# Bidirectional selective scan with a routed FFN gate on one core: two more states scaled on ScalarE, two more products with C on GpSimd, and a new table of steps

## The reference

```
xn = layernorm(x)                                   # over channels
def scan(x, x_proj_w, dt_proj_w, dt_proj_b, A_log, Dp):
    A = -exp(A_log)                                 # 256 channels x 16 states
    delta, B, C = split(x @ x_proj_w.T)             # 32 + 16 + 16
    delta = softplus(delta @ dt_proj_w.T + dt_proj_b)
    h[t] = exp(delta[t]*A) * h[t-1] + delta[t]*B[t]*x[t]     # per channel and state
    return sum over states of h*C  + Dp*x
s = scan(xn, forward weights) + reverse(scan(reverse(xn), backward weights))
g = silu(xn + 0.3*(expert(xn) @ Wo + bo))           # one of 8 experts per batch: W2 @ gelu(W1 @ xn)
out = x + s*g
```

## Time and profile before

| | |
|---|---|
| profiled execution / its span | 3351.6 / 3349.7 us |
| TensorE busy | 2571.1 us, 77% |
| VectorE busy | 3109.2 us, 93% |
| ScalarE busy | 2909.8 us, 87% |
| GpSimd busy | 3010.5 us, 90% |
| DMA, share of 16 engines | 38.3% |
| mean granted clock of TensorE | 0.91 |

### The profile page before, as it was taken

One profiled execution on the slowest core, in us unless ns is written; L12 is line 12 of the kernel. 1 busy time (PEld: TensorE's weight loads), 2 busy tenths in 40 slices (PEclk: granted clock), 3 DMA queues, 4 the chain that ended last, 5 costly groups with the idle time before them and its releaser, 6 DMA issues. The chain is left out here.

```text
span 3349.7 us, 47861 instructions
## 1 busy us (share of the span) xinstructions
PE 2571.1 (77%) x15542; PEld 2055.5 (61%) x15542; DVE 3109.2 (93%) x2059; ACT 2909.8 (87%) x5370; POOL 3010.5 (90%) x1422
## 2 busy tenths in 40 slices
PE   7677777777778777777777787777787777778776
PEld 4566566666566666666665666665666666666665
DVE  2799999999999999999999999999999999999999
ACT  3898898988898898899888899988988988988885
POOL 0889999999999999999899999999999999999997
PEclk8898899889998988899898999889998988998898
DMA  5333434433434433434324444334344334344232
GB/s 171 112 110 94 131 121 129 127 106 96 139 121 128 125 99 105 136 120 128 114 87 131 126 132 125 107 98 131 121 128 125 105 99 138 121 129 125 95 104 70
DMA packets 273358, 394.09 MB, mean 118 GB/s; under 512 B 45003, under 2 KB 119508, under 8 KB 273108
## 3 DMA queue, kind: packets, MB, share of 16 engines
q1 hardware_dynamic: 273108, 391.03, 38.3%
HBM read 348.98 MB, written 25.18 MB: 112 GB/s over the span
## 5 line engine op out<-in xcount | busy, mean ns | idle before, releaser
L452 POOL TENSOR_TENSOR bx<-dx,b_sb 128x1024 f32<-128x1024 f32 x640 | 1514.5, 2386 | 75.9 <-DVE hs L798 75.3
L798 DVE TENSOR_TENSOR_SCAN hs<-decay,bx 128x1024 f32<-128x1024 f32 x640 | 1457.1, 2279 | 53.5 <-ACT decay L696 40.1
L1032 PE MATMUL y<-ident,hc 128*128 128x128 f32 x8192 | 1144.8, 291 | 29.1 <-DVE hc L776 29.0
L1032 PEld LDWEIGHTS y<-ident,hc 128*128 128x128 f32 x8192 | 1029.2, 152 | 144.6 <-DVE hc L776 85.7
L440 POOL TENSOR_TENSOR hc<-hs,c_sb 128x1024 f32<-128x1024 f32 x416 | 983.2, 2376 | 7.3 <-DVE hs L798 7.3
L798 DVE TENSOR_TENSOR_SCAN hs<-decay_sb,decay 128x1024 f32<-128x1024 f32 x384 | 864.8, 2273 | 76.9 <-issue 37.8
L699 ACT ACTIVATE decay<-delta,rate 128x512 f32<-128x512 f32 (+1 forms) x1280 | 827.2, 683 | 64.0 <-DVE hs L798 63.5
L776 DVE TENSOR_TENSOR hc<-hs,c 128x1024 f32<-128x1024 f32 x608 | 728.3, 1198 | 38.2 <-PE c L1015 32.4
L561 ACT ACTIVATE dxb<-dxT,btok 128x256 f32<-128x256 f32 x1536 | 651.1, 497 | 0.0
L1007 PE MATMUL decay<-ident,dxb 128*128 128x128 f32 x3072 | 443.7, 292 | 248.9 <-DVE hs L798 244.4
L1007 PEld LDWEIGHTS decay<-ident,dxb 128*128 128x128 f32 x3072 | 367.1, 149 | 363.7 <-issue 269.4
(11 more groups left out here) (127 smaller groups left out, 2287.7 us busy)
## 6 DMA issues: line engine op xcount, KB each, us to landing
b_sb<-b_scratch SPq DMA_DIRECT2D x640, 256.0 KB, 3.3
c_sb<-b_scratch SPq DMA_DIRECT2D x416, 256.0 KB, 3.5
xin<-in_L_attn_x_dram SPq DMA_DIRECT2D x32, 512.0 KB, 7.6
w_sb<-in_L_ffn_W_dram SPq DMA_DIRECT2D x32, 512.0 KB
w2o_sb<-w2o_scratch SPq DMA_DIRECT2D x32, 512.0 KB
xres<-in_L_attn_x_dram SPq DMA_DIRECT2D x32, 512.0 KB, 5.3
out_dram<-og SPq DMA_DIRECT2D x32, 512.0 KB, 4.3
dbc<-high SPq DMA_DIRECT2D x64, 128.0 KB, 5.4
```

The source lines that it names most:

```text
L452: nc.gpsimd.tensor_tensor(bx[:, i % RING, :, :], dx[:, g, :, :], b_sb[:, i % BRING, :].unsqueeze(1).broadcast_to([P, DT, T]), ALU.mult).th ...
L798: V.tensor_tensor_scan(hs[:, s % HSLOTS, :, :].rearrange("p k t -> p (k t)")[:, u], factor.rearrange("p k t -> p (k t)")[:, u], data.rearr ...
L1032: ins = M(yps[:, c, k * P:(k + 1) * P], hc[:, s % RING, k, c * P:(c + 1) * P], ident[:, :], start=False, stop=(s == ADDED[-1]), is_transpo ...
```

## The change

Only numbers of the table change. Two more states are `TURNED` (14 for 12: 20 and 26 come in; `POOL_B` falls from 20 to 18), and `POOL_C` grows from 13 to 15, other states than before among them; VectorE's products fall from 19 to 17 a row. `MEAN`, `SCALE`, `SHIFT` go from steps 0, 1, 4 to 1, 3, 5, the second `RATIO` from 30 to 35, the second `LOG1P` from 36 to 38, the first two `DX_COPY` from 30, 31 to 32, 33.

```diff
-    MEAN, SCALE, SHIFT, NORM = 0, 1, 4, 6
+    MEAN, SCALE, SHIFT, NORM = 1, 3, 5, 6
-    EXPAND, ABS = (14, 15, 24, 25), (16, 17, 26, 27)
-    EXP, LN, SQUARE, RATIO = (18, 27), (19, 28), (20, 29), (21, 30)
-    LOG1P, STEPSIZE, DX = (25, 36), (27, 39), (28, 43)
-    DX_TURN, DX_COPY = (28, 29, 44, 45), (30, 31, 46, 47)
-    FFN_IN, HIDDEN, GELU = (16, 16, 18, 18, 20, 20, 22, 22), (18, 20, 22, 24), 31
+    EXPAND, ABS = (14, 16, 26, 27), (17, 19, 29, 30)
+    EXP, LN, SQUARE, RATIO = (20, 30), (21, 31), (22, 34), (23, 35)
+    LOG1P, STEPSIZE, DX = (25, 38), (27, 40), (28, 43)
+    DX_TURN, DX_COPY = (28, 29, 44, 45), (32, 33, 46, 47)
+    FFN_IN, HIDDEN, GELU = (18, 18, 20, 20, 22, 22, 24, 24), (21, 23, 25, 27), 31
-    TURNED = (5, 6, 8, 9, 11, 13, 14, 15, 22, 24, 28, 30)
-    SCALED_AT = (0, 2, 3, 4, 5, 7, 9, 10, 17, 19, 23, 25)
+    TURNED = (5, 6, 8, 9, 11, 13, 14, 15, 20, 22, 24, 26, 28, 30)
+    SCALED_AT = (1, 2, 3, 4, 5, 7, 9, 10, 16, 17, 18, 20, 22, 24)
-    POOL_C = (2, 4, 5, 7, 9, 10, 11, 12, 16, 18, 20, 26, 27)
+    POOL_C = (1, 3, 5, 6, 9, 10, 11, 12, 14, 16, 18, 19, 20, 22, 26)
```

More of the change, by code:

```diff
@@ L47, in mamba_moe_block @@
     SKIP = {0: ((0, 0), (2, 0)), 1: ((0, 1), (1, 0), (1, 1), (2, 1)), 4: ((3, 0), (3, 1))}
-    TURNED, SCALED_AT, TURN_LEAD = (5, 6, 8, 9, 11, 13, 14, 15, 22, 24, 28, 30), (0, 2, 3, 4, 5, 7, 9, 10, 17, 19, 23, 25), 3
+    TURNED, SCALED_AT, TURN_LEAD = (5, 6, 8, 9, 11, 13, 14, 15, 20, 22, 24, 26, 28, 30), (1, 2, 3, 4, 5, 7, 9, 10, 16, 17, 18, 20, 22, 24), 3
     POOL_B = [s for s in range(STEPS) if s not in TURNED]
-    POOL_C, C_LAG, ADD_LAG = (2, 4, 5, 7, 9, 10, 11, 12, 16, 18, 20, 26, 27), 4, 2
+    POOL_C, C_LAG, ADD_LAG = (1, 3, 5, 6, 9, 10, 11, 12, 14, 16, 18, 19, 20, 22, 26), 4, 2
     ON_DVE = [s for s in range(STEPS) if s not in POOL_C]
```

## The result

The changed kernel takes 4025.74 us (median of four runs, 4022.52 to 4027.28), the kernel before 3361.25 us on the same chip (3357.11 to 3365.94): the ratio is 1.1966, 95% interval 1.1946 to 1.1987. The forecast was 3930 us with a range of 3710 to 4040. It is slower, by the loop that was forecast, and 96 us more than forecast. The profiled execution has a span of 4020.7 us.

What follows compares the result with a forecast made beforehand. VectorE was taken to bound the kernel, with 4.8 us idle a row. A row of 107.2 + 12.3 = 119.5 us, 18.5 over 101.0, gave +573 over 31 seams: 3925, plus 5.8, so 3930 us, range 3710 to 4040.

Steps and rivals of the forecast that it cites:

- the loop that was forecast: Late waits in series leading from one row to the next: a row of 119.5 us, 18.5 more than 101.0.
- T: The end of scan 0, from which the prediction counts its times; 1729.6 in the rows of before.
- seam: VectorE, end of scan 31 to end of the next row's scan 0: 12.3 us, where it was 6.35.
- step 2: GpSimd's small operations to the expansion of delta: transfers into dbc come later, expansion at T + 60.8 (58.7 to 64.9).
- the bound at the late end: The latest landing of a transfer into dbc in step 2, 8.5 us at most: 4058 us in all.
- Step 1: T to GpSimd's four small operations: rsq ready at T + 17.3, GpSimd waits 12.7 us, VectorE stalls 7 us.
- Step 3: Softplus of the first direction: RATIO ends at T + 84.3, GpSimd's LOG1P waits 5 us more.
- rival A: Faster: waits between engines give way, only VectorE's two products count; 98.7 us a row, 3286 us; chance 0.04.
- Rival B: Only the seam counts, GpSimd's list not late: +3.65 a row, 3470 us; chance 0.1, shared with one stall alone.
- C: Slower by GpSimd late from Step 1 and the seam, dbc and RATIO in time: 3770 us; chance 0.2.
- Rival D: TensorE becomes the bound, its clock falling in idle time: perhaps 2 to 3 us a row, 3990 to 4020; chance 0.1.
- The Trainium skill's drain behind a table load: About 1.38 us at each table load; by this rule seam 15.1, row 2.8 us longer; the forecast left it out.

Runs made afterwards that it cites:

- dbc_early: The changed kernel with SyncE's transfers into dbc issued ahead of the loads of C and of x: 3851.97 us.
- csd_log: copy_scale_dbc with the two LOG1P at 27 and 39 instead of 25 and 38 and the first STEPSIZE at 28: 3338.84 us, ratio 0.9921.
- copy_scale_dbc: The changed kernel with the first two dx copies at 31, 32, MEAN, SCALE, SHIFT at 0, 1, 4, and the edit of dbc_early: 3488.86 us.

## Why the prediction was right

**The mechanism** was right, and its places in time came out, up to the transfers into dbc and in the pieces behind them: T + 17.4 for the small operations (forecast 17.4), T + 27.8 for C product 3 (27.8), T + 53.4 for C product 12 (53.5), 22.8 us of softplus (22.7), a seam of 12.7 (12.3), and 23.1 us between the start of LOG1P at 1667.16 and the end of scan 31 (22.9). The experiments show the parts as causes and not only as rows: removed one by one and together they add.

**The size** was 96 us short, and the term that was mis-sized is in step 2: "a transfer lands 5.5 us after", of which I took 4.4 because there would be less traffic. That median is over all 128 transfers, but TensorE waits for the last of four, and in the row shown that took 7.2 us (1759.34 to 1766.56). The median of the fourth transfer alone, from issue to landing, is 6.9 us in the trace of the kernel before and 6.6 after, so the trace had it. The expansion came at T + 63.5 and not T + 60.8. ScalarE read the bank 1.2 us later and not 0.75, as TensorE's matmuls ran at a granted clock of 0.50 there (0.76 us for 0.48 at 1.00): it began at T + 64.7 in the row shown and not at T + 61.6. With 0.3 us more from LOG1P to the end of scan 31 and 0.4 at the seam, a steady row became 123.1 and not 119.5.

Two errors in the count of rows lie over this, of opposite sign. The first row also runs through the loop up to its own last operation, which came at 227.9 and not at 211.6: 16 us that "31 seams" left out. But the last of the 31 intervals, counted like the others, takes 97.0 us (92.0 before), since no front of a next row stands in it, and the one ahead of it 119.0: 23 us that the sum had too much. 29 x 3.6 - 23 + 16 = 97. That the last row hid 23 us of the miss is luck; the bound at the late end, 8.5 us for the transfer, held the rest.

**Step 1** had one thing hidden in it: undoing it alone gave 132 us and not 221, since the second RATIO, moved to 35, stands in the same step. The stall of 6.3 us at scan 7 had two causes, one behind the other. The prediction counted RATIO as a part of the delay of `rsq`, not as a wait of its own.

**Step 3** is borne out in kind. GpSimd's wait for RATIO was 7.4 us a row, (299.3 - 62.5)/32, where the prediction had 5.2 (T + 84.3 less T + 79.1). Of it 4.7 went with dbc_early: they were the late transfers. Only 2.7 are the two steps between RATIO and LOG1P by themselves. The 150 us of csd_log look like the forecast's 5.2 x 31 = 161, but csd_log moves both LOG1P, and the waits in copy_scale_dbc divide about evenly between the two. The second one is not in step 3; in the changed kernel it hides behind the wait for rsq.

**Busy time as the rival A read it** (98.7 us a row) didn't come in any kernel. The best, csd_log, has (3331.0 - 206.2)/31 = 100.8 us; of VectorE's 2.3 us fewer a small part came out, 0.2 us by this row and (3363.47 - 3338.84)/31 = 0.8 by the medians on one chip. Its scans wait 72.4 us where the profile names no releaser, up from 43.8 in the kernel before; what these waits are was not tried and stays open.

**Rival B and C**: decay 4 did wait for scan 2 as said, and dbc was not in time. **Rival D**: the mean granted clock fell from 0.91 to 0.84, and C after the idle time took 0.78 us for 0.48, but this is some 0.8 us a row at the seam and 0.5 at the expansion of delta, not 2 to 3.

The Trainium skill's drain behind a table load ("ScalarE: Activation LUTs", section "What ACT_TABLE_LOAD costs") doesn't show after the change either: the load ends at 1694.12 and GELU starts at 1694.13, the next load ends at 1697.34 and the copy starts at 1697.35. The seam of 12.7 has no room for 2.8 us more.

## What to carry to other kernels

When engines walk in order through one table of steps, a step number isn't a time: to move a unit, follow for each engine what it waits for ahead of that unit, and look for the loop that leads from one row back to itself. A copy that another engine's queue waits for must not stand behind an operation that waits for that queue's result, and above all not behind a table load. Leave at least as many steps between producer and consumer as the engines are apart; two and three steps between RATIO and the two LOG1P cost 150 us against four at both. Four are no rule either: they left GpSimd no wait in csd_log, and 1.5 us a row in the kernel before, so look at the wait and not at the step number. A queue that serves several consumers (SyncE's here) has to be checked when a list changes, since a load that isn't urgent can hold up one that is.

## What the runs showed of the hardware

The last of four transfers of 128 KB issued 0.6 us apart was used only 7.2 us after its start, when the median from issue to landing over all of them is 5.5 us (before) and 5.6 (after). By their place in the four the medians after are 5.1, 5.5, 5.9 and 6.6 us, and before 5.2, 5.4, 5.6 and 6.9. TensorE's matmul that took 0.48 us at a granted clock of 1.00 took 0.76 at 0.50, where it came after 9 us of idle time. Nothing else went against what the rows of the kernel before had shown.
